# Four GNN layers over 64 graphs: row sums by way of DRAM, natural unit order, other weight loads first, variance groups of four slots

## The chip, the core and the metric

The kernel runs on one core of a Trainium2 chip. The metric is the device time of one execution, in microseconds; the median of three runs stands for a kernel. The engines are named as in the profile: PE (TensorE matmul; PEld is its weight load), DVE (VectorE), ACT (ScalarE), POOL (GpSimd) and SP, whose queue issues all DMAs here.

## The reference

There are 64 graphs of 128 nodes with 128 features, each with a dense 128x128 adjacency matrix, and four GNN layers with a layer norm after each. The cost is in the first layer, which makes a hidden vector for every pair of nodes:

```python
hi = einsum('bsh,hk->bsk', x, W1[:H]); hj = einsum('bsh,hk->bsk', x, W1[H:])
h = relu(hi[:, :, None, :] + hj[:, None, :, :] + b1)      # 128 x 128 pairs of 128 values a graph
y = einsum('bijk,kl->bijl', h, W2) + b2
y = layernorm(y) * gamma + beta                           # over the last axis, for every pair
out = einsum('bij,bijh->bih', adj, y)
...
x = _layernorm(x + L0(x, adj)); x = _layernorm(x + L1(x, adj))
x = _layernorm(x + L2(x, adj)); x = _layernorm(x + L3(x, adj))   # L3 has three such layers inside
```

## The kernel before

**Units and slots.** For a node i, the unit i is the 128x128 tile of h for all j (features on partitions). A graph has 128 units, worked on eight at a time: a slot (16 a graph). Each engine's program is one long list by slots; between its own steps of the first layer it carries the later layers of older graphs (the tail), placed by a table `AT` of slot and ninth of a slot (lines 88 to 101). Engines meet only through semaphores. An engine runs its list in order, so a wait holds all that stands behind it. A stage named with lag L does slot t of a graph in program slot t + L.

**The first layer.** ACT, POOL and DVE make the units of slot t at lag 4 (`START`): `hidden`, lines 556, 924 and 669. POOL makes two units of a slot, or three in the slots of `ROOTLESS`; DVE one in every second slot and four in the last; ACT the rest, five or so. The units go to a ring `h` of 18 slots. PE multiplies the eight units by W2 less its mean in two blocks of 512 columns (`products`, line 417, lag 5), into two PSUM buffers in turn. ACT squares the result (`squares`, line 566, lag 6) into a ring `sq` of four slots. PE sums the squares over the features by matmuls with a one-hot column into `ss_ps` (`variances`, line 429): once in two slots, four matmuls of 512 columns, one to each quarter of 32 output columns. Each fp32 matmul shows as two records. After eight slots ACT takes the square root (`deviations`, line 573), SP's DMAs straighten the rows (line 324), DVE inverts them (693) and multiplies by the adjacency values (`coefficients`, line 701), which also gives a row sum in `c_row_sum`. The coefficients go to DRAM (335) and come back copied to all partitions (347, 349). DVE then sums each unit of h weighted with them (`weighted_sum`, line 685, a custom operation and a read of its accumulator, lag 19), 14 slots behind the products.

**Row sums.** The first layer adds for each node the sum of its coefficients times a bias. The two columns of `c_row_sum` hold half rows in an order of units that groups them by quarter (`unit_of`, line 75). DVE copies them (869), PE brings them to node order with two one-column matmuls against the matrices `row_pick` (`c_sum_mm`, line 450), and DVE copies the result (740), used at line 744.

**Norms.** DVE takes mean and variance (709, 712), POOL adds eps and raises to the power -0.5 (912, 915), DVE applies it (718 or 792) six ninths of a slot after the variance.

**Loads.** SP loads x, then seven weights counted on one semaphore `weights_in`, in the order W1 (two halves), b1, W2, b2 twice, gamma. ACT, DVE and PE wait for all seven. PE starts `make_uv` (402, 403), from which all units come, after DVE has centred W2 and made the affine terms (808 to 821). In each graph SP issues eight DMAs of 32 partitions for `adj_c` (288), then the tail's inputs (358, 359).

## Time and profile before

| | us |
|---|---|
| median of 3 runs (2756.32 to 2757.82) | 2756.94 |
| the profiled execution | 2755.1 |
| its span, first to last instruction | 2753.5 |

PE is busy for 98% of the span, DVE 95%, ACT 93%, POOL 90%. The granted clock of TensorE is at full speed in all slices but the last (nine tenths or more against five), where only the tail is left. A graph takes some 41.9 us in the long middle part. Since all four engines are near full, the busy share alone doesn't tell which sets the pace; the waits and the timeline do. In the profile an instruction's duration includes its way through the pipeline, so neighbours overlap: what a step costs an engine is read from start to start.

### The profile page before, as it was taken

To read this page: it belongs to the slowest core of one execution; us is meant where nothing else is said; L and a number is where in the kernel's file an instruction comes from. 1 tells how busy PE (TensorE), PEld (TensorE's weight loads), DVE (VectorE), ACT (ScalarE), POOL (GpSimd) and SP (SyncE) were. 2 spreads that over 40 slices of the span, in tenths; PEclk is the share of its full clock that TensorE was granted. 3 is DMA by queue.
4 is the path that set the end of the run, shared out by engine and by line. 5 is a ranking of instruction groups with operands and counts; after the bars stand their busy time and mean duration, and the time that the engine had idled before them with its cause. 6 is when DMAs were issued, how large, how long until landed. Compare 5 with 4: busy or idle time off the path is not lost.

```text
span 2753.5 us, 60836 instructions
## 1 busy us (share of the span) xinstructions
PE 2690.3 (98%) x10882; PEld 1147.3 (42%) x10882; DVE 2619.0 (95%) x20102; ACT 2567.7 (93%) x6903; POOL 2487.8 (90%) x3498
## 2 busy tenths in 40 slices
PE   8999999999999999999999999999999999999993
PEld 2344444444444444444444444444444444444442
DVE  4999999999999999999999999999999999999997
ACT  7999999999999999999999999999999999999991
POOL 3899999999999999999999999999999999999992
PEclk9999999999999999999999999999999999999995
DMA  3655655655555555556556555555655565565562
GB/s 108 237 196 209 231 206 196 231 219 194 215 231 201 202 226 219 197 215 231 199 200 232 214 194 221 227 199 203 230 213 197 214 236 196 202 234 210 195 228 95
DMA packets 188668, 571.72 MB, mean 208 GB/s; under 512 B 70656, under 2 KB 106368, under 8 KB 139136
## 3 DMA queue, kind: packets, MB, share of 16 engines
q1 hardware_dynamic: 188288, 567.83, 54.5%
q14 instruction: 285, 2.33, 0.3%
q8 instruction: 95, 1.56, 0.2%
HBM read 555.17 MB, written 8.39 MB: 205 GB/s over the span
## 4 chain that ended last, share of the span: by engine, by line
PE 67%; ACT 18%; DVE 8%; issue 6%; POOL 1%; DMA 0%; SPq 0%; ACTq 0%; DVEq 0%; POOLq 0%
PE y_ps L417 47%; PE ss_ps L429 13%; ACT h L556 11%; DVE h L685 5%; ACT sq L566 4%; ACT dev_rows L573 2%; PE prod_bank L479 1%; PE prod_bank L483 1%; PE prod_bank L450 1%; ACT hid L595 1%; PE prod_bank L456 1%; PE prod_bank L457 1%; PE uv_ps L402 1%; PE uv_ps L403 1%; POOL h L924 1%
## 5 line engine op out<-in xcount | busy, mean ns | idle before, releaser
L924 POOL TENSOR_SCALAR h<-vT,uT 128x128 f32<-128x128 f32 x2520 | 2056.7, 831 | 23.7 <-ACT vT L546 23.3
L417 PE MATMUL y_ps<-h,w2c 128*128 128x512 f32 x4096 | 2016.4, 609 | 11.4 <-DVE h L669 1.6
L685 DVE CUSTOM_DVE_ANT_0 h<-h,cb 128x128 f32<-128x128 f32 x8192 | 1983.9, 289 | 10.0 <-DVE gT_keep L749 0.5
L556 ACT ACTIVATE h<-uv_ps,uT 128x128 f32<-128x128 f32 x4848 | 1409.2, 433 | 0.0
L566 ACT ACTIVATE sq<-y_ps,b2c_col 128x1024 f32<-128x1024 f32 x1024 | 1182.5, 1155 | 112.3 <-PE y_ps L417 112.1
L417 PEld LDWEIGHTS y_ps<-h,w2c 128*128 128x128 f32 x4096 | 682.2, 190 | 903.6 <-issue 723.7
L685 DVE DVE_READ_ACCUMULATOR2_ANT gT<- 128x1 f32 x8192 | 636.8, 78 | 0.1
L429 PE MATMUL ss_ps<-sq,sel 128*32 128x512 f32 x4096 | 545.5, 605 | 0.9 <-ACT sq L566 0.9
L915 POOL TENSOR_TENSOR rs<-var_eps,minus_half 128x1 f32<-128x1 f32 x448 | 302.7, 676 | 35.1
L669 DVE TENSOR_SCALAR h<-vT,uT 128x128 f32<-128x128 f32 x757 | 200.9, 294 | 4.7 <-ACT mask_all L611 2.6
L912 POOL TENSOR_TENSOR var_eps<-mv,eps_col 128x1 f32<-128x1 f32 x448 | 96.1, 215 | 117.9 <-DVE mv L712 115.0
L429 PEld LDWEIGHTS ss_ps<-sq,sel 128*32 128x32 f32 x4096 | 80.6, 108 | 225.5 <-ACT sq L566 105.0
L709 DVE BATCH_NORM_STATS2 stats<-z 128x6 f32<-128x128 f32 x448 | 127.4, 284 | 0.3
L483 PEld LDWEIGHTS prod_bank<-l3w,aggT 128*128 128x128 f32 x384 | 73.6, 194 | 93.0 <-issue 58.6
L693 DVE RECIPROCAL invs<-devs 128x64 f32<-128x64 f32 x128 | 70.1, 548 | 38.6 <-DMA devs<-dev_rows 35.6
L718 DVE TENSOR_SCALAR x<-z,mv,rs 128x128 f32<-128x128 f32 x256 | 96.7, 378 | 6.2 <-POOL rs L915 4.8
L907 POOL TENSOR_TENSOR dis_raw<-degree_floor,minus_half 128x1 f32<-128x1 f32 x64 | 35.1, 548 | 65.3 <-DVE degree_floor L733 65.3
L599 ACT ACTIVATE aggT<-prod_bank 128x128 f32<-128x128 f32 x192 | 66.3, 345 | 25.3 <-PE prod_bank L479 21.7
L604 ACT ACTIVATE h<-z_aff 128x128 f32<-128x128 f32 x192 | 70.4, 367 | 17.5 <-DVE z_aff L792 17.5
L792 DVE SCALAR_TENSOR_TENSOR z_aff<-z_aff,rs,l3beta 128x128 f32<-128x128 f32 x192 | 81.9, 427 | 4.6 <-POOL rs L915 2.9
L573 ACT ACTIVATE dev_rows<-ss_ps 128x512 f32<-128x512 f32 x128 | 79.8, 624 | 1.2 <-PE ss_ps L429 1.2
L712 DVE BATCH_NORM_AGGREGATE mv<-stats 128x2 f32<-128x6 f32 x448 | 77.8, 174 | 2.6
(100 smaller groups left out, 1489.8 us busy)
## 6 DMA issues: line engine op xcount, KB each, us to landing
cb<-c_scratch SPq DMA_DIRECT2D x384, 1024.0 KB, 9.3
cb<-c_scratch SPq DMA_DIRECT2D x256, 512.0 KB, 4.8
adj_c<-in_adj_dram SPq DMA_DIRECT2D x512, 8.0 KB
devs<-dev_rows SPq DMA_DIRECT2D x512, 8.0 KB
x_in<-in_x_dram SPq DMA_DIRECT2D x64, 64.0 KB, 10.8
c_scratch<-c SPq DMA_DIRECT2D x128, 32.0 KB, 1.5
adj_in<-in_adj_dram SPq DMA_DIRECT2D x64, 64.0 KB, 4.4
x_res<-in_x_dram SPq DMA_DIRECT2D x64, 64.0 KB, 5.4
```

What stands on the lines that cost most here:

```text
L417: op = pe.matmul(y_ps[:, t % 2, c0:c0 + COLS], w2c[:], h[:, (SLOTS * g + t) % H_RING, c0:c0 + COLS], start=True, stop=True)
L429: mm = pe.matmul(ss_ps[32 * q:32 * q + 32, :], sel[:, ROWS - 1 - p:ROWS - 1 - p + 32], sq[:, (t + q // 2) % SQ_RING, c0:c0 + COLS], start= ...
L483: pe.matmul(out, aggT[:, b, :], l3w[:, i, :], start=True, stop=False)
L556: op = act.activation(h[:, (SLOTS * g + t) % H_RING, n * P:(n + 1) * P], v, ACT.Relu, bias=uT[:, b, i:i + 1])
L566: act.activation(sq[:, t % SQ_RING, :], y_ps[:, t % 2, :], ACT.Square, bias=b2c_col[:], scale=float(P) ** -0.5).then_inc(sq_done, 1)
L573: act.activation(dev_rows[:, half, :], ss_ps[:], ACT.Sqrt, bias=EPS).then_inc(dev_done, 1)
L669: op = dve.tensor_scalar(h[:, (SLOTS * g + t) % H_RING, n * P:(n + 1) * P], vT[:, b, :], uT[:, b, i:i + 1], 0.0, ALU.add, ALU.max)
L685: op = dve.tensor_tensor_reduce(h[:, (SLOTS * g + t) % H_RING, cols], h[:, (SLOTS * g + t) % H_RING, cols], cb[:, t // 2, c0:c0 + P], 1.0, ...
L709: dve.bn_stats(stats[:, b, :], z[:, b, :]).then_inc(stats_set[name], 1)
L718: dve.tensor_scalar(dst[:, b, :], z[:, b, :], mv[:, b, 0:1], rs[:, b:b + 1], ALU.subtract, ALU.mult).then_inc(normed[name], 1)
L915: pool.tensor_tensor(rs[:, b:b + 1], var_eps[:, b:b + 1], minus_half[:], ALU.pow).then_inc(rs_set[name], 1)
L924: op = pool.tensor_scalar(h[:, (SLOTS * g + t) % H_RING, n * P:(n + 1) * P], vT[:, b, :], uT[:, b, i:i + 1], 0.0, ALU.add, ALU.max)
```

## The change

1. **Natural order.** `unit_of` becomes `8 t + n`. The adjacency values of a half are then one contiguous piece, loaded with one DMA of 128 partitions instead of four of 32.
2. **Row sums through DRAM.** After each store of coefficients SP stores the half's `c_row_sum` (4 bytes a partition) to DRAM, and `load_row_sums` brings both halves back as pairs `c_pair`, of which DVE adds the two. The copy at 869, `row_pick` and the matmuls at 450 go.
3. **Variance groups.** `variances` runs once in four slots with 8 matmuls; `sq` has five slots. `products` moves from one to two slots behind the units (lag 6), squares to lag 7, variances to lag 10, sums to lag 20, and `h` has 19 slots. The tail's steps move by about a slot; `l0_sum` stands two ninths later against `l0_mm`.
4. **POOL.** `ROOTLESS` has nine slots: POOL makes 41 units a graph instead of 40, ACT 76 instead of 77.
5. **Start.** W2 is loaded first, with a semaphore of its own, then W1 and b1 with `w1_in`; PE waits for these alone, and DVE's work on b2 and gamma moves behind its first four units. PE's waits for the later weights' set-up move two slots on.
6. **Last graph.** Its norms no longer use POOL: ACT takes the root of variance plus eps, DVE the reciprocal.

```diff
-TTR_LAG = START + 15
-H_RING = 18
+PRODUCT_LAG = START + 2
+TTR_LAG = START + 16
+H_RING = 19
-SQ_RING = 4
-ROOTLESS = (1, 2, 3, 5, 7, 9, 11, 14)
+SQ_RING = 5
+GROUP = 4
+ROOTLESS = (1, 2, 3, 4, 5, 8, 10, 12, 15)
...
-    half, b = t // HALF, 2 * (t % HALF) + n // BLOCK_UNITS
-    return 64 * half + 16 * (b % 4) + 4 * (b // 4) + n % BLOCK_UNITS
+    return DUO_UNITS * t + n
...
-    ("g_keep", 3, 4), ("l0_mm", 4, 0), ("l0_sum", 4, 5), ("ln0", 4, 6), ("x1_scaled", 5, 6),
+    ("g_keep", 4, 4), ("l0_mm", 5, 0), ("l0_sum", 5, 7), ("ln0", 5, 8), ("x1_scaled", 6, 7),
...
             def load_adj_c_rows(a):
-                rows = a.rearrange("(h q p n) (l j) -> h p q (n l) j", h=2, q=4, p=CHUNKS, l=2)
+                rows = a.rearrange("(h i) (l j) -> h (i l) j", h=2, l=2)
                 for half in range(2):
-                    for p in range(CHUNKS):
-                        sp.dma_start(adj_c[32 * p:32 * p + 32, half, :], rows[half, p]).then_inc(adj_c_in, 16)
+                    sp.dma_start(adj_c[:, half, :], rows[half]).then_inc(adj_c_in, 16)
...
+                wait_apart(sp, c_pair_in, 16 * g)
+                wait_apart(sp, rows_stored[half], 16 * g)
+                sp.dma_start(rows_dram[half].rearrange("(p o) -> p o", o=1), c_row_sum[:, half:half + 1]
+                             ).then_inc(rows_stored[half], 16)
+
+            def load_row_sums(g, b):
+
+                for half in range(2):
+                    wait_apart(sp, rows_stored[half], 16 * (g + 1))
+                wait_apart(sp, c_sum_set, g - 1)
+                wait_apart(sp, c_pair_in, 16 * g)
+                sp.dma_start(c_pair[:, b, :], rows_dram.rearrange("h (i l) -> (h i) l", l=2)).then_inc(c_pair_in, 16)
...
                     spread_coefficients(old, 1)
+                    load_row_sums(old, 1 - buf)
...
             def variances(g, t):
 
-                half, p = t // HALF, (t % HALF) // 2
-                wait(pe, sq_done, SLOTS * g + t + 2)
-                if p == 0:
+                half = t // HALF
+                wait(pe, sq_done, SLOTS * g + t + GROUP)
+                if t % HALF == 0:
                     wait(pe, dev_done, 2 * g + half)
-                for q in range(4):
-                    c0 = (q % 2) * COLS
-                    mm = pe.matmul(ss_ps[32 * q:32 * q + 32, :], sel[:, ROWS - 1 - p:ROWS - 1 - p + 32],
-                                   sq[:, (t + q // 2) % SQ_RING, c0:c0 + COLS],
-                                   start=(p == 0), stop=(p == ROWS - 1))
+                for d in range(GROUP):
+                    p = (t + d) % HALF // 2
+                    for block in range(2):
+                        q = 2 * (d % 2) + block
+                        mm = pe.matmul(ss_ps[32 * q:32 * q + 32, :], sel[:, ROWS - 1 - p:ROWS - 1 - p + 32],
+                                       sq[:, (SLOTS * g + t + d) % SQ_RING, block * COLS:(block + 1) * COLS],
+                                       start=(p == 0), stop=(p == ROWS - 1))
                 mm.then_inc(var_summed, 1)
...
-                if due("c_sum_mm"):
-                    wait(pe, rows_kept, g + 1)
-                    wait(pe, adjT_set, g + 1)
-                    for half in range(2):
-                        op = pe.matmul(c_sum_ps[b], row_pick[:, half, :], rows_sum[:, half:half + 1],
-                                       start=(half == 0), stop=(half == 1))
-                    op.then_inc(c_summed, 1)
...
-            pe.wait_ge(weights_in, 16 * WEIGHTS)
-            pe.wait_ge(w2c_set, 1)
-            pe.wait_ge(affine_set, 2)
+            pe.wait_ge(w1_in, 16 * FIRST_WEIGHTS)
...
-                    sg, t = lagging(graphs, s, START + 3)
-                    if s % 2 == 1 and sg is not None:
+                    sg, t = lagging(graphs, s, PRODUCT_LAG + GROUP)
+                    if t % GROUP == 0 and sg is not None:
                         variances(sg, t)
...
+                for name in NORMS:
+                    if g == G - 1 and lo <= AT[name] + 2 < hi:
+                        wait(act, mv_set[name], g + 1)
+                        act.activation(var_eps[:, b:b + 1], mv[:, b, 1:2], ACT.Sqrt, bias=EPS).then_inc(eps_added[name], 1)
...
+                if g == G - 1 and lo <= at + NORM_AT - 1 < hi:
+                    wait(dve, eps_added[name], g + 1)
+                    dve.reciprocal(rs[:, b:b + 1], var_eps[:, b:b + 1]).then_inc(rs_set[name], 1)
...
-                        if ct == HALF + 1 and cg is not None and k == FINE - 1:
-                            wait(dve, c_made, 2 * (cg + 1))
-                            wait(dve, c_summed, cg)
-                            dve.tensor_copy(rows_sum[:], c_row_sum[:]).then_inc(rows_kept, 1)
```

**On PE**, in a graph of the long middle part, from the row sums to the first layer's end (`y_ps` is a product block, `ss_ps` a variance matmul, `x4` or `x8` how many stand in a row, `uv_ps` the two matmuls of `make_uv`). Before:

```order
L417 MATMUL y_ps<-h,w2c 128x512 x3
L450 MATMUL prod_bank<-rows_sum,row_pick 128x1 x2
L429 MATMUL ss_ps<-sq,sel 32x512 x4
L417 MATMUL y_ps<-h,w2c 128x512 x3
L402 MATMUL uv_ps<-xT,w1a 128x128
L403 MATMUL uv_ps<-xT,w1b 128x128
L417 MATMUL y_ps<-h,w2c 128x512
L429 MATMUL ss_ps<-sq,sel 32x512 x4
```

Now:

```order
L438 MATMUL y_ps<-h,w2c 128x512 x5
L452 MATMUL ss_ps<-sq,sel 32x512 x8
L438 MATMUL y_ps<-h,w2c 128x512
L421 MATMUL uv_ps<-xT,w1a 128x128
L422 MATMUL uv_ps<-xT,w1b 128x128
L438 MATMUL y_ps<-h,w2c 128x512 x4
L472 MATMUL prod_bank<-w2cg,gT_keep 128x128
```

Two groups of four have become one of eight, with one product block between it and `uv_ps` instead of three, and the row-sum matmuls are gone.

**On SP's queue**, from the store of the second half's coefficients to the tail's inputs (`c_scratch` is the store, `cb` the copies to all partitions). Before:

```order
L335 DMA c_scratch<-c 128x64 [waits cb_in7,cb_in6,cb_first1,cb_in5,c_stored1,cb_in4,c_made]
L347 DMA cb<-c_scratch 128x1024 [waits ttr_done,c_stored1]
L349 DMA cb<-c_scratch 128x1024
L349 DMA cb<-c_scratch 128x2048 [waits ttr_done] x3
L288 DMA adj_c<-in_adj_dram 32x1x64 [waits adj_c_in,c_made]
L288 DMA adj_c<-in_adj_dram 32x1x64 x7
L358 DMA adj_in<-in_adj_dram 128x128 [waits x_base_set,tail_in,degree_set,l3_agged2]
```

Now:

```order
L341 DMA c_scratch<-c 128x64 [waits cb_in7,cb_in6,cb_first1,cb_in5,c_stored1,cb_in4,c_made]
L345 DMA row_sum_scratch<-c_row_sum 128x1 [waits rows_stored1,c_pair_in]
L365 DMA cb<-c_scratch 128x1024 [waits ttr_done,c_stored1]
L367 DMA cb<-c_scratch 128x1024
L367 DMA cb<-c_scratch 128x2048 [waits ttr_done] x3
L354 DMA c_pair<-row_sum_scratch 128x2 [waits c_sum_set,c_pair_in,rows_stored1,rows_stored0]
L290 DMA adj_c<-in_adj_dram 128x64 [waits adj_c_in,c_made]
L290 DMA adj_c<-in_adj_dram 128x64
L376 DMA adj_in<-in_adj_dram 128x128 [waits x_base_set,tail_in,degree_set,l3_agged2]
```

A small store stands ahead of the copies, a small load behind them, and six of eight `adj_c` issues are gone.

## Rows read from the trace of the kernel before

**Rows 1.** busy time of each engine over the whole span:

```profile
PE 2690.3 (98%) x10882; PEld 1147.3 (42%) x10882; DVE 2619.0 (95%) x20102; ACT 2567.7 (93%) x6903; POOL 2487.8 (90%) x3498
```

**Rows 2.** the chain of waits that ended last, shares of the span by line:

```profile
PE y_ps L417 47%; PE ss_ps L429 13%; ACT h L556 11%; DVE h L685 5%; ACT sq L566 4%; ACT dev_rows L573 2%; PE prod_bank L479 1%; PE prod_bank L483 1%; PE prod_bank L450 1%; ACT hid L595 1%; PE prod_bank L456 1%; PE prod_bank L457 1%; PE uv_ps L402 1%; PE uv_ps L403 1%; POOL h L924 1%
```

**Rows 3.** busy us of PE, PEld, DVE, ACT, POOL in fifty graphs:

```profile
507.06:2600.11 2093.05, 2087.41 (x8501) 891.02 (x8500) 2031.58 (x15652) 2004.34 (x5401) 1963.56 (x2751) 1.00 0.56 213
```

**Rows 4.** waits in those fifty graphs: us in total, times, longest us:

```profile
PEld y_ps L417 <- ACT h L556: 121.1, 350, 0.4
ACT sq L566 <- PE y_ps L417: 85.7, 200, 0.7
DVE z L753 <- PE prod_bank L457: 32.8, 49, 0.8
DVE invs L693 <- DMA devs<-dev_rows: 8.4, 31, 1.4
```

**Rows 5.** timeline of DVE: start us, duration us, instruction:

```profile
89.21 0.31 DVE L749 COPY gT_keep<-gT 128x128 f32<-128x128 f32 x1
...
507.06 0.31 DVE L749 COPY gT_keep<-gT 128x128 f32<-128x128 f32 x1
...
2600.11 0.31 DVE L749 COPY gT_keep<-gT 128x128 f32<-128x128 f32 x1
...
2683.65 0.31 DVE L749 COPY gT_keep<-gT 128x128 f32<-128x128 f32 x1
```

**Rows 6.** timeline of PE around a variance group and the next:

```profile
1408.51 1.06 PE L429 MATMUL ss_ps<-sq,sel 128*32 128x512 f32 x8
1409.51 1.98 PE L417 MATMUL y_ps<-h,w2c 128*128 128x512 f32 x4
1411.33 0.27 PE L395 MATMUL prod_bank<-ident,x_in 128*128 128x128 f32 x1
1411.44 1.88 PE L417 MATMUL y_ps<-h,w2c 128*128 128x512 f32 x4
1413.16 0.38 PE L479 MATMUL prod_bank<-adj_in,x 128*128 128x128 f32 x2
1413.47 1.06 PE L429 MATMUL ss_ps<-sq,sel 128*32 128x512 f32 x8
```

**Rows 7.** timeline of PE at the row-sum matmuls:

```profile
1423.40 0.50 PE L450 MATMUL prod_bank<-rows_sum,row_pick 128*128 128x1 f32 x4
1423.83 1.07 PE L429 MATMUL ss_ps<-sq,sel 128*32 128x512 f32 x8
```

**Rows 8.** costliest lines, whole span: operation, count | busy us, mean ns | idle:

```profile
L924 POOL TENSOR_SCALAR h<-vT,uT 128x128 f32<-128x128 f32 x2520 | 2056.7, 831 | 23.7 <-ACT vT L546 23.3
...
L685 DVE CUSTOM_DVE_ANT_0 h<-h,cb 128x128 f32<-128x128 f32 x8192 | 1983.9, 289 | 10.0 <-DVE gT_keep L749 0.5
```

**Rows 9.** the same view of DVE alone, 2708 to 2720 us:

```profile
L685 DVE CUSTOM_DVE_ANT_0 h<-h,cb 128x128 f32<-128x128 f32 x47 | 10.7, 282 | 0.0
```

**Rows 10.** timeline of SP's queue and DVE, from row-sum source to its use:

```profile
1405.01 5.37 SPq L288 DMA_DIRECT2D adj_c<-in_adj_dram  x8
...
1424.24 0.08 DVE L685 DVE_READ_ACCUMULATOR2_ANT gT<- 128x1 f32 x1
```

**Rows 11.** timeline of the start:

```profile
2.58 0.43 SPq L297 DMA_DIRECT2D w<-in_L_gnn_W_dram  x1
...
9.38 0.77 PE L402 MATMUL uv_ps<-xT,w1a 128*128 128x128 f32 x2 [6.17 <-DVE b2cg L821]
```

**Rows 12.** DMA issues: size of one, median us from issue to landing:

```profile
b_col<-in_L_gnn_b_dram SPq DMA_DIRECT2D x2, 0.5 KB, 2.8
```

**Rows 13.** timeline of a layer norm in the last graph's tail:

```profile
2727.62 0.18 DVE L712 BATCH_NORM_AGGREGATE mv<-stats 128x2 f32<-128x6 f32 x1
...
2727.88 0.19 POOL L912 TENSOR_TENSOR var_eps<-mv,eps_col 128x1 f32<-128x1 f32 x1 [1.71 <-DVE mv L712]
...
2728.73 0.34 DVE L718 TENSOR_SCALAR x<-z,mv,rs 128x128 f32<-128x128 f32 x1 [0.93 <-POOL rs L915]
```

100 lines of the change are left out of this document (54 added, 46 removed), and 16 rows, old and new, of the table AT.

## The prediction

> **What bounds the kernel now.** I read the busy shares first, then the chain of waits, then the waits and the timeline of fifty graphs from the middle. PE is busy for 98% of the span [rows 1], and the chain that ended last lies for 47% on the products and 13% on the variance matmuls [rows 2]. A graph takes (2600.11 - 507.06) / 50 = 41.86 us, and the same over all 62 steps from the first copy of `gT` to the last but one, (2683.65 - 89.21) / 62 = 41.85 [rows 5]. In these fifty graphs PE shows 2087.41 us busy of 2093.05, DVE 2031.58, ACT 2004.34, POOL 1963.56 [rows 3]: a graph costs PE 41.75 us, DVE 40.63, ACT 40.09, POOL 39.27. ACT's idle time is nearly all waiting for a product, 85.7 us or 1.7 a graph; the weight loads of PE wait 121.1 us for units of ACT, but mostly while the matmul before still streams [rows 4]. So PE sets the pace, with some coupling to ACT, and DVE is right behind it. DVE's two large waits, for `z` (32.8 us) and for the deviations (8.4), are 0.82 us a graph [rows 4]. Without them DVE would need 41.86 - 0.82 = 41.04 us. That is the wall behind PE: whatever PE gains beyond 0.8 us a graph is lost unless DVE gains too.
>
> **Variance groups.** A group starts at 1408.51 and the next product at 1409.51, 1.00 us; eight records over four quarters of the columns are two steps of about 0.43 (four products in a row take 1413.16 - 1411.44 = 1.72), so 0.14 of it is start and end. The four product matmuls behind the group take 1411.33 - 1409.51 = 1.82, 0.10 more than the others. Ahead of the group two short matmuls take 0.31 (1413.16 to 1413.47); I take 0.09 of this as the switch to quarters, an estimate [rows 6]. Each group thus costs 0.33 us beside its streaming. Four of eight per graph go, if the second half of a doubled group streams straight on: 1.3 us less on PE. If it doesn't, only the switches go, 4 x 0.19 = 0.8. If the two halves cost as now and more waits come, nothing.
>
> **Row sums.** PE's two matmuls hold it from 1423.40 to 1423.83, 0.43 us [rows 7]; without them the group's own 0.09 comes back, so 0.34 less. PE then needs 41.75 - 1.3 - 0.3 = 40.1 us a graph and drops under DVE. DVE loses one small copy; the similar one at 740 lasts 0.15 us [rows 10], of which I count 0.1. The other becomes an addition of the same size, no change. The load of the pairs is issued where the `adj_c` loads start now, at 1405.01, and its sum is used at about 1424.24: 19 us of cover [rows 10] against 2.8 us for the landing of a like column [rows 12], plus what the copies ahead of it take. If the cover failed, DVE would stand for the excess and all sums behind it. The small store ahead of the copies takes SP one issue, 0.43 us by the nearest [rows 11], and the copies wait for the coefficients' landing beside it anyway. I price it at 0, with 0.4 us a half as its bound, which the three slots from coefficients to first sum would cover. Two `adj_c` issues instead of eight free the queue of about 4 us out of 5.37 [rows 10], worth nothing, since the tail's loads are not waited for.
>
> **Units and lags.** ACT gives one unit a graph to POOL: 0.43 us long on ACT at most, 0.83 on POOL [rows 8], which then needs 39.27 + 0.83 = 40.1 of its 41. The second slot between units and products takes away PE's waits for ACT's last unit. It does not loosen the loop between products and squares, with only two buffers in PSUM; the doubled group sits in it (a rival below). Products and sums move together, 14 slots apart as before, so the end of the first layer after the last product stays; one more slot of units ahead of products at the start costs up to a slot, 41.85 / 16 = 2.6 us, but ACT is idle there. I take +1. `l0_sum` gets two more ninths of a slot, which takes off most of the 32.8 us.
>
> **Start.** PE now starts `make_uv` at 9.38 us, after all seven weights and DVE's set-up. In the new order b1 is the fifth issue, where one starts at 2.58 now [rows 11], and such a column lands 2.8 us later [rows 12]: 5.4 us. So -4.0, all on the path since nothing else can start. The bound is 0, if POOL's set-up, which waits for the later weights, takes the lead in the second graph.
>
> **Last graph.** From the start of the variance operation to its use in a norm it is 2728.73 - 2727.62 = 1.11 us, with two POOL operations of 0.19 and 0.55 between [rows 13]. One column on ACT and one on DVE I estimate at 0.25 and 0.15, and with hand-offs as here 0.76 in all. Seven norms save 7 x 0.35 = 2.4; some overlap with another graph's, so -2 (0 to -3.5).
>
> **The sum.** Against the profiled execution (2755.1, span 2753.5, 1.6 around it): DVE as the new bound at 41.04 - 0.1 = 40.9, plus 0.1 of waits that stay, makes 41.0 us a graph. 62 x (41.85 - 41.0) = 53 less; -4 start, +1 lag, -2 tail: -58, so 2697 for that execution. It stands 1.8 under the median, so 2756.9 - 58 = **2699**.
>
> **A rule against it.** At the same time in which POOL's units run, DVE's sums last 289 ns on average [rows 8]; with POOL nearly idle at the end they last 282 [rows 9]. All of POOL's 40 units cost DVE's 128 sums 128 x 7 ns = 0.9 us, so one more costs 0.02. DVE at 97% and POOL at 94% busy together [rows 3] leave no room for turns. The Trainium skill's page "SBUF — State Buffer", section "SBUF: two separate sides", says that a VectorE operation with two SBUF inputs and a GpSimd operation that reads SBUF hold one port pair in turn, each blocked for the whole of the other; the trace does not agree for these. If POOL's added unit held DVE up for its full 0.83 us, DVE would need 40.9 + 0.8 = 41.7 and the graphs would gain 9 us at most, which with the ends gives 2743: a chance of 3%.
>
> **Rivals.**
> (a) *The loop of products and squares* takes the place of the bound. From the end of the square that a group waits for: group 1.9 with its switch, next product block 1.82 plus 0.2 to 0.4 of tail matmuls and 0.15 for the last one's end [rows 6], then ACT three squares and two rounds of five units, 3 x 1.0 + 2 x 1.4 (estimates from 40.09 / 16 = 2.5 us a slot, rows 3). That is 9.9 to 10.1 us for four slots, against 10.25 at 41.0 a graph. Nearly level: jitter can take it to 10.35, 41.4 a graph, 62 x 0.45 + 5 = 33 less, **2724**. The same time comes out if POOL, with 0.9 us of slack left, is late with a norm's factor and DVE waits for it. For it speaks that all four engines would be within 1 us of each other; against it that ACT has 1.7 us of waiting to give and the tail matmuls behind three of the four groups are one or none. Chance 23%.
> (b) *Slower*: the same loop, with a doubled group that restarts between its halves (2.1 with the switch) and a square that is late behind ACT's square root of the deviations in two of four groups. The loop exceeds 10.46 us, at which nothing is gained; at 10.6 a graph takes 42.3, 62 x 0.45 = 28 more, less 5: **2780**. It decides from 0.4 us over my sum for the loop. Chance 8%.
> (c) *The groups give only the switches, or the waits move to `z`*: 41.7 a graph, 62 x 0.15 + 5 = 14 less, or the loop just cancels the rest: **2743 to 2755**. Chance 8%, half of it within 0.2%. That the row sums come late and cancel the gain is in here too, at 1%.
> (d) *DVE gains too*: many of its gaps under 0.15 us, 0.4 us a graph in all (61.5 us of idle time in rows 3 less the 41.2 of rows 4, over 50), are short waits for a PE that is late. With PE ahead they go: 40.6 a graph, 62 x 0.4 = 25 less than forecast, **2674**. Chance 13%.
>
> **How the numbers follow.** Forecast 45% (2685 to 2712), (a) 23%, (d) 13%, (b) 8%, (c) 8%, the port rule 3%. The range leaves out (b), the upper end of (c) and the outermost of (d): 2676 to 2744. Faster by over 0.2% (about what a measurement here can tell from no change), under 2751: 45 + 23 + 13 + 3 + half of (c) = 0.87, of which I keep 0.86. Within 0.2%: 0.05. Slower: 0.09.
>
> **What would show it.** Right: `gT` copies 41.0 us apart; DVE busy over 98% in the middle with its wait for `z` at 753 nearly gone; a variance group of 16 records about 1.85 us long; PE's weight loads without waits for ACT's units; the first product at about 8.2 us; `c_pair` never waited for. ACT's waits for products fewer but longer, behind groups. Wrong: groups over 2.0 us long, DVE idle over 1 us a graph on `prod_bank` or POOL's `rs`, or ACT waiting over 2 us a graph for products.

## The result and the profile after

| | us |
|---|---|
| the kernel before, median in the same comparison | 2757.2 |
| the changed kernel, median of 4 runs (3389.52 to 3405.39) | 3401.9 |
| ratio, with its 95% interval | 1.233 (1.231 to 1.235) |
| the profiled execution of after / its span | 3404.1 / 3402.3 |

The forecast was 2699, with 2676 to 2744 as its range. The change makes the kernel 23% slower, by 645 us. One execution of all runs below, of e19, was slow (6088.7 us, where its other three took 2707.6 to 2709.4); e19's time is the median of those three.

Busy time of each engine over the whole span of after, which answers to [rows 1]:

```profile
PE 2904.3 (85%) x10626; PEld 1213.7 (36%) x10626; DVE 2583.3 (76%) x20042; ACT 2569.7 (76%) x6847; POOL 2500.3 (73%) x3547
```

The chain of waits that ended last, by engine and by line, against [rows 2]:

```profile
DMA 48%; DVE 36%; PE 8%; SPq 4%; issue 3%; ACT 1%; DVEq 0%; POOL 0%; ACTq 0%
DMA cb<-c_scratch 33%; DVE h L709 22%; DMA x_res<-in_x_dram 11%; DMA c_scratch<-c 4%; PE y_ps L438 3%; PE ss_ps L452 3%; SPq L367 2%; DVE gT L709 2%; DVE stats L733 2%; DVE z_aff L820 1%; DVE h L693 1%; DVE z_aff L815 1%; DVE z L807 1%; DVE invs L717 1%; SPq L290 1%
```

No engine is near full, and DVE, ACT and POOL have about the same work as before. The chain has gone from PE to a DMA: a third of it is `cb<-c_scratch`, the copy of the coefficients to all partitions; another 11% is the load of the tail's `x_res`, which lands in 10.4 us instead of 5.4. The weighted sums (line 709 now, 685 before), among the costliest lines, against [rows 8]:

```profile
L709 DVE CUSTOM_DVE_ANT_0 h<-h,cb 128x128 f32<-128x128 f32 x8192 | 1975.9, 289 | 669.8 <-DMA cb<-c_scratch 669.3
```

An operation lasts 289 ns, as before, but DVE stands 669 us waiting for the copies, against 10.0 us of idle time before these operations in [rows 8]. That is as long as the whole loss, 10.5 us a graph. The copies' own rows (KB each, median us from issue to landing) in after:

```profile
cb<-c_scratch SPq DMA_DIRECT2D x384, 1024.0 KB, 14.3
cb<-c_scratch SPq DMA_DIRECT2D x256, 512.0 KB, 11.9
```

and in the kernel before:

```profile
cb<-c_scratch SPq DMA_DIRECT2D x384, 1024.0 KB, 9.3
cb<-c_scratch SPq DMA_DIRECT2D x256, 512.0 KB, 4.8
```

The same copies land 5 to 7 us later. SP's queue shows what stands ahead of them. After, one half of a graph (start us, duration us, instruction; 341 stores the coefficients, 345 is the new store of the row sums, 365 and 367 issue the copies):

```profile
1538.98 0.33 SPq L341 DMA_DIRECT2D c_scratch<-c  x1
1539.40 0.38 SPq L345 DMA_DIRECT2D row_sum_scratch<-c_row_sum  x1
1540.45 0.32 SPq L365 DMA_DIRECT2D cb<-c_scratch  x1
1540.82 9.21 SPq L367 DMA_DIRECT2D cb<-c_scratch  x4
```

The same view of the kernel before:

```profile
1400.01 0.32 SPq L335 DMA_DIRECT2D c_scratch<-c  x1
1401.50 0.33 SPq L347 DMA_DIRECT2D cb<-c_scratch  x1
1401.88 3.03 SPq L349 DMA_DIRECT2D cb<-c_scratch  x4
```

In both the first copy is issued 1.5 us behind the store of the coefficients, once that has landed (in after 1.4 us in the median; a single one took 5.7). What is late is the first copy's own landing, first after (line 365), then before (line 347):

```profile
DMA to landing us min/median/max: 6.8/11.3/12.5
DMA to landing us min/median/max: 3.7/4.0/5.4
```

The four copies behind it take 9.21 us to issue instead of 3.03, but that follows from the delay in good part: SP waits for DVE's sums to free the buffers. Its waits for them, after and before (us in total, times, longest):

```profile
SPq L367 <- DVE gT L709: 580.8, 184, 5.5
SPq L349 <- DVE gT L685: 20.3, 69, 0.6
```

On DVE's side of the half shown:

```profile
1552.11 0.29 DVE L709 CUSTOM_DVE_ANT_0 h<-h,cb 128x128 f32<-128x128 f32 x1 [5.41 <-DMA cb<-c_scratch]
```

Fifty graphs in the middle of after, between two copies of `gT` (first the us; then busy us of PE, PEld, DVE, ACT, POOL; the granted clock as a share of full speed; DMA share; GB/s), against [rows 3]:

```profile
614.11:3220.19 2606.08, 2260.13 (x8304) 943.82 (x8302) 2003.36 (x15601) 2005.69 (x5356) 1977.72 (x2801) 0.91 0.61 171
```

A graph takes 52.12 us instead of 41.86. The granted clock is 0.91, where it was 1.00: TensorE's clock spends part of the time at the lower of its two levels, 1.2 instead of 2.4 GHz, while PE now stands idle in every graph, which it did not before. PE's busy time grows from 2087 to 2260 us, but PE still has over 300 us to spare, and DVE's wait for the copies is as long as the loss, so I take the clock as a consequence; no run changes it alone.

### The profile page after: what moved, and what is told of

It is laid out like the page before. It is cut to its first block, busy times and chain, and to the rows that moved or that the text cites. A ratio compares the mean times of both kernels' runs of the same rounds, so it can differ in the third digit from the quotient of the medians.

```text
span 3402.3 us, 60251 instructions
## 1 busy us (share of the span) xinstructions
PE 2904.3 (85%) x10626; PEld 1213.7 (36%) x10626; DVE 2583.3 (76%) x20042; ACT 2569.7 (76%) x6847; POOL 2500.3 (73%) x3547
## 4 chain that ended last, share of the span: by engine, by line
DMA 48%; DVE 36%; PE 8%; SPq 4%; issue 3%; ACT 1%; DVEq 0%; POOL 0%; ACTq 0%
DMA cb<-c_scratch 33%; DVE h L709 22%; DMA x_res<-in_x_dram 11%; DMA c_scratch<-c 4%; PE y_ps L438 3%; PE ss_ps L452 3%; SPq L367 2%; DVE gT L709 2%; DVE stats L733 2%; DVE z_aff L820 1%; DVE h L693 1%; DVE z_aff L815 1%; DVE z L807 1%; DVE invs L717 1%; SPq L290 1%
## 5 line engine op out<-in xcount | busy, mean ns | idle before, releaser
L438 PE MATMUL y_ps<-h,w2c 128*128 128x512 f32 x4096 | 2125.0, 643 | 70.1 <-DVE h L693 60.8
L438 PEld LDWEIGHTS y_ps<-h,w2c 128*128 128x128 f32 x4096 | 748.7, 205 | 958.3 <-issue 733.4
L452 PE MATMUL ss_ps<-sq,sel 128*32 128x512 f32 x4096 | 572.9, 683 | 1.4 <-ACT sq L587 1.2
L495 PE MATMUL prod_bank<-adj_in,x 128*128 128x128 f32 x128 | 40.9, 412 | 228.9 <-DVE x L746 228.9
L452 PEld LDWEIGHTS ss_ps<-sq,sel 128*32 128x32 f32 x4096 | 115.3, 117 | 306.2 <-issue 189.3
L477 PE MATMUL prod_bank<-adjT,x1s 128*128 128x128 f32 x128 | 45.3, 451 | 155.5 <-DVE x1s L787 155.5
L613 ACT ACTIVATE aggT<-prod_bank 128x128 f32<-128x128 f32 x64 | 17.8, 278 | 188.4 <-PE prod_bank L477 188.4
L495 PEld LDWEIGHTS prod_bank<-adj_in,x 128*128 128x128 f32 x128 | 25.3, 247 | 281.0 <-DVE x L746 281.0
L477 PEld LDWEIGHTS prod_bank<-adjT,x1s 128*128 128x128 f32 x128 | 28.1, 274 | 209.2 <-DVE x1s L787 209.2
L499 PE MATMUL prod_bank<-l3w,aggT 128*128 128x128 f32 x384 | 83.6, 300 | 3.5 <-ACT aggT L624 3.4
## 6 DMA issues: line engine op xcount, KB each, us to landing
cb<-c_scratch SPq DMA_DIRECT2D x384, 1024.0 KB, 14.3
cb<-c_scratch SPq DMA_DIRECT2D x256, 512.0 KB, 11.9
adj_c<-in_adj_dram SPq DMA_DIRECT2D x128, 32.0 KB, 10.4
x_res<-in_x_dram SPq DMA_DIRECT2D x64, 64.0 KB, 10.4
```

Of the source, the lines that this page charges most:

```text
L438: op = pe.matmul(y_ps[:, t % 2, c0:c0 + COLS], w2c[:], h[:, (SLOTS * g + t) % H_RING, c0:c0 + COLS], start=True, stop=True)
L452: mm = pe.matmul(ss_ps[32 * q:32 * q + 32, :], sel[:, ROWS - 1 - p:ROWS - 1 - p + 32], sq[:, (SLOTS * g + t + d) % SQ_RING, block * COLS:( ...
L499: pe.matmul(out, aggT[:, b, :], l3w[:, i, :], start=True, stop=False)
```

## The experiments

Times are medians; ratios are against the kernel before on the same chip, with 95% intervals. A graph's time is taken from the first copy of `gT` to the last but one, over 62. The diffs are against the kernel named ahead of them and cut to their core.

### What makes the copies late

**e1, row sums on PE.** The changed kernel with its row sums made as before, by two one-column matmuls (with a `row_pick` for the natural order), and nothing sent through DRAM.

```diff
-                sp.dma_start(rows_dram[half].rearrange("(p o) -> p o", o=1), c_row_sum[:, half:half + 1]
-                             ).then_inc(rows_stored[half], 16)
...
+                if due("c_sum_mm"):
+                    wait(pe, rows_kept, g + 1)
...
+                        op = pe.matmul(c_sum_ps[b], row_pick[:, half, :], rows_sum[:, half:half + 1],
+                                       start=(half == 0), stop=(half == 1))
```

> The changed kernel with the row sums made as before (a copy on VectorE, two one-column matmuls against a pick matrix in natural order, a copy back) and no row-sum DMAs; all else of the change stays. Theory S (the small stores): the 4-byte stores of the row sums hold back the copies of the coefficients by about 5 us twice a graph, and nothing else is slow. Then this run loses the whole of it and shows what the rest of the change is worth, by my forecast less the 0.3 us a graph of the two matmuls, which are back on PE: 2699 to 2720 us, and VectorE's wait for the copies is under 10 us in all instead of 669. Rival G (the groups): the bursts of eight variance matmuls or the new order of loads of the adjacency values are the cause; then it stays over 3200 us.

Measured: 2786.2, ratio 1.011 (1.009 to 1.013), 42.51 us a graph. The way through DRAM costs 616 of the 645 us. But what is left isn't 2699 to 2720: there is a second loss, beyond what this run was expected to show.

**e2, the stores alone.** The kernel before with nothing added but a 4-byte store per partition and half, right behind the store of the coefficients. Nobody reads what is stored. DVE also waits for the previous graph's store before it overwrites the column; e8 below has the same wait.

```diff
+        rows_dram = nc.dram_tensor("row_sum_scratch", (2, P), F32, kind="Internal").ap()
...
                 sp.dma_start(c_dram[half].rearrange("(b j) -> b j", j=SPAN), c[:, half, :]
                              ).then_inc(c_stored[half], 16)
+                wait_apart(sp, rows_stored[half], 16 * g)
+                sp.dma_start(rows_dram[half].rearrange("(p o) -> p o", o=1), c_row_sum[:, half:half + 1]
+                             ).then_inc(rows_stored[half], 16)
```

> The kernel before with one thing added: the store of the half's row sums (128 rows of 4 bytes) to DRAM behind each store of coefficients; nothing reads it. Theory S: about 5 us twice a graph, less the slack of the copies in the kernel before (their wait was 0.5 us in all, so the slack is unknown): 3250 to 3400 us. Rival G: 2757 to 2765 us, since one more issue on SP's queue costs nothing.

Measured: 3358.0, ratio 1.219 (1.216 to 1.221), 51.26 us a graph. Its waits (us in total, times, longest) and the landing of its copies:

```profile
DVE h L692 <- DMA cb<-c_scratch: 639.7, 136, 6.3
```

```profile
cb<-c_scratch SPq DMA_DIRECT2D x384, 1024.0 KB, 14.1
cb<-c_scratch SPq DMA_DIRECT2D x256, 512.0 KB, 11.9
```

Two stores of 512 bytes a graph, in a kernel otherwise unchanged, cost 603 us, 4.7 us each, with the same late copies. Neither the load of the pairs, the natural order nor the lags are needed for it.

**e3, the stores behind the copies.** In the changed kernel each store of row sums is issued behind the half's copies.

```diff
                     spread_coefficients(old, 0)
+                    store_row_sums(old, 0)
...
                     spread_coefficients(old, 1)
+                    store_row_sums(old, 1)
                     load_row_sums(old, 1 - buf)
```

> The changed kernel with the row-sum stores moved behind the copies of the same half on SP's queue; same DMAs, other order. Theory S, in the form that the stores only hold up what stands behind them: the copies of the coefficients run as before, only the loads of the adjacency values and of the tail come about 5 us later, with 19 us of cover: 2690 to 2760 us. In the form that the stores disturb all reads in flight, the copies that are still running are slowed: 2900 to 3400 us. Rival G: 3400 us.

Measured: 3201.3, ratio 1.162 (1.159 to 1.164), 48.82 us a graph. That lies in the range given for the second form of S, but its mechanism is not there: the copies land as in the kernel before (9.3 and 4.8 us). The first form, that only what stands behind the stores is late, fits what follows, but the delay is far over the 5 us that it took. The landing of the stores, SP's longest wait, and one of DVE's:

```profile
row_sum_scratch<-c_row_sum SPq DMA_DIRECT2D x128, 0.5 KB, 14.7
```

```profile
SPq L245 <- DMA row_sum_scratch<-c_row_sum: 910.0, 64, 15.6
```

```profile
DVE degree L761 <- DMA x_res<-in_x_dram: 367.3, 64, 9.1
```

SP stands 14.2 us a graph for the store's landing before it can load the pairs; the next graph's `adj_c` and the tail's loads are issued behind that, and DVE waits 5.7 us a graph for the tail's `x_res`. The slow store now hurts whoever is queued behind it. Putting it elsewhere in the queue moves the bill and doesn't pay it.

**e4, 512 bytes apart.** The changed kernel, each row sum at its own 512 bytes of DRAM.

```diff
-        rows_dram = nc.dram_tensor("row_sum_scratch", (2, P), F32, kind="Internal").ap()
+        rows_dram = nc.dram_tensor("row_sum_scratch", (2, P, P), F32, kind="Internal").ap()
```

> The changed kernel with each row sum stored 512 bytes from the next in DRAM (and gathered from there), so no two of the 4-byte writes share a 512-byte piece. Theory S with many writes to the same piece of memory as the cause: the delay goes, 2690 to 2800 us. Theory S with small writes as such as the cause: 3300 to 3450 us, as now. Rival G: 3400 us.

Measured: 2782.0, ratio 1.010 (1.008 to 1.012), 42.43 us a graph. The same 128 values in the same place of the queue now land in

```profile
row_sum_scratch<-c_row_sum SPq DMA_DIRECT2D x128, 0.5 KB, 1.5
```

and the copies in 9.3 and 4.8 us again. 620 us of 645 are gone, with all else as in the change.

**e8, 64 bytes apart.** The run e2 with the unread values 64 bytes apart.

```diff
-        rows_dram = nc.dram_tensor("row_sum_scratch", (2, P), F32, kind="Internal").ap()
+        rows_dram = nc.dram_tensor("row_sum_scratch", (2, P, 16), F32, kind="Internal").ap()
```

> The kernel of the run e2 (before plus the unused row-sum stores) with the 128 values of a store 64 bytes apart in DRAM instead of 4. If the cost comes from many writes to the same 64 bytes: 2755 to 2800 us. If it comes from writes to the same larger piece (512 bytes or more): the copies stay late, though less often, 2900 to 3360 us.

Measured: 2756.2, ratio 1.000 (0.999 to 1.001), 41.85 us a graph. As many DMAs, packets and bytes as in e2, and nothing of its 603 us is left. It isn't the small size of a piece of data that costs, nor the issue; it is that 128 separate 4-byte writes go to neighbouring addresses. The Trainium skill's page "DMA: Bandwidth & Descriptors", section "Specifications", says that transfers under 512 bytes are done by read-modify-write. The trace agrees that such a store can be dear, but the rule alone would charge e2 and e8 alike, and the store of the coefficients, 256 bytes a row, lands in 1.5 us in both. What happens in the memory no run shows, nor what a spacing between 4 and 64 bytes would give.

### What keeps the repaired change slower than before

Without the slow store the change is at 2782 to 2787, 83 to 88 us over the forecast. Two theories: P, that POOL with its 41st unit has become late; L, the loop of products and squares, lengthened by the doubled variance group (rivals (a) and (b)). In e1 the chain lies for 54% on POOL, which speaks for P.

**e5, 40 units for POOL**, and **e6, 38 units**, both as e1 else.

```diff
-ROOTLESS = (1, 2, 3, 4, 5, 8, 10, 12, 15)
+ROOTLESS = (2, 3, 4, 5, 8, 10, 12, 15)
```

```diff
-ROOTLESS = (1, 2, 3, 4, 5, 8, 10, 12, 15)
+ROOTLESS = (3, 5, 8, 10, 12, 15)
```

> The kernel of the run e1 (the change with row sums on PE) with POOL back at 40 units a graph, slot 1 out of the list of slots with three. In e1 the chain that ended last lies 54% on POOL and a graph takes 42.54 us. Theory P (POOL's 41st unit is what still makes it slower than before): a unit of POOL with its gap, 0.87 us a graph, goes: 41.7 us a graph or less, 2725 to 2735 us, and POOL's share of the chain falls under 20%. Rival L (the longer lags or the doubled variance group cost the time, and POOL only waits with the others): 2780 to 2790 us, with another engine in the chain.

> As e5 with 38 units on POOL and 79 on ACT. Theory P: POOL leaves the chain, the next bound is VectorE at 40.9 to 41.0 us a graph or the loop of squares and products with ACT 0.5 us fuller: 2685 to 2715 us. If ACT takes over as the bound, 2720 to 2760. Rival L: 2780 us or more.

Measured: e5 2786.9, ratio 1.011 (1.009 to 1.013), no gain at all; e6 2770.5, 1.005 (1.004 to 1.007), which lies in none of the three ranges expected. In e5 the chain has only changed its engines:

```profile
ACT 34%; DVE 22%; PE 19%; POOL 15%; issue 9%; DMA 0%; SPq 0%; DVEq 0%; POOLq 0%; ACTq 0%
```

So P falls for the 41st unit: POOL's large share in e1 didn't mean that taking it off would help. e6's 16 us are looked at again below. One doubled group on PE's timeline in e5, and on ACT's the square that waits for the product behind it:

```profile
1417.52 1.92 PE L439 MATMUL ss_ps<-sq,sel 128*32 128x512 f32 x16
1419.38 1.98 PE L425 MATMUL y_ps<-h,w2c 128*128 128x512 f32 x4
```

```profile
1418.30 1.56 ACT L570 ACTIVATE h<-uv_ps,uT 128x128 f32<-128x128 f32 x5
1421.40 1.11 ACT L582 ACTIVATE sq<-y_ps,b2c_col 128x1024 f32<-128x1024 f32 x1 [1.53 <-PE y_ps L425]
```

The group holds PE for 1.86 us; the next slot's product is whole only at 1421.4, and ACT, done with its units at 1419.87, stands 1.53 us. A square that is late can then hold a later group. Groups in e6:

```profile
1409.04 1.92 PE L439 MATMUL ss_ps<-sq,sel 128*32 128x512 f32 x16
...
1419.13 1.92 PE L439 MATMUL ss_ps<-sq,sel 128*32 128x512 f32 x16
...
1429.58 1.92 PE L439 MATMUL ss_ps<-sq,sel 128*32 128x512 f32 x16 [0.25 <-ACT sq L582]
...
1440.21 1.92 PE L439 MATMUL ss_ps<-sq,sel 128*32 128x512 f32 x16
```

They are 10.09, 10.45 and 10.63 us apart, and the group behind them starts at 1451.27, 11.06 later. Wanted were 10.25, and rival (a) summed up 9.9 to 10.1; the mean over the run is 42.25 / 4 = 10.56. The spacings differ with the tail's matmuls between them, so the mean counts and not one of them.

**e7, the 41st unit in the kernel before.**

```diff
-ROOTLESS = (1, 2, 3, 5, 7, 9, 11, 14)
+ROOTLESS = (1, 2, 3, 5, 6, 7, 9, 11, 14)
```

> The kernel before with one unit a graph moved from ACT to POOL (slot 6 added to the slots with three), nothing else. Theory P in its plain form: POOL has 2.6 us idle in 41.9, but must be on time for the norms, so the unit costs a part of its 0.87 us: 2770 to 2800 us. If POOL's idle time covers it, 2750 to 2760 us, and it is the new schedule that made POOL's time dear.

Measured: 2756.6, ratio 1.000 (0.999 to 1.001). Free there, as counted.

**e9, groups of two slots.** e5 with the variance matmuls in groups of two slots again; lags, order and tables stay.

```diff
-SQ_RING = 5
-GROUP = 4
+SQ_RING = 4
+GROUP = 2
```

> The kernel of the run e5 (row sums and 40 units as before, products two slots behind the units) with variance groups of two slots and a ring of four squares, as before. Theory B (the loop: square, then the doubled group, then the next products, then squares again, with only two product buffers, is longer than a slot's time allows): with groups of two the loop has 0.9 us less in it, and the second slot of lag takes away PE's waits for ACT's units: 41.3 to 41.9 us a graph, 2710 to 2750 us. Rival L (the longer lags cost the time): 2775 us or more.

Measured: 2748.2, ratio 0.997 (0.996 to 0.999), 41.88 us a graph. The doubled group costs at least 38.7 us at lag two: e9's chain lies for 70% on POOL, so something else holds it there.

**e11 and e12, lag one.** e5 with the lags, rings, table of the tail's steps and `ROOTLESS` of the kernel before, with groups of four (e11) and of two (e12).

```diff
-PRODUCT_LAG = START + 2
-TTR_LAG = START + 16
-H_RING = 19
+PRODUCT_LAG = START + 1
+TTR_LAG = START + 15
+H_RING = 18
...
-ROOTLESS = (2, 3, 4, 5, 8, 10, 12, 15)
+ROOTLESS = (1, 2, 3, 5, 7, 9, 11, 14)
```

> The kernel of the run e5 with the lags, the ring of 18 slots and the table of the tail as before (products one slot behind the units), and variance groups of four. Theory B: the same loop is in it, and a product block waits for ACT's last unit besides: 2785 us or more. Rival L: 2700 to 2750 us.

> Lags and groups as before together: what is left of the change is the natural order, W2 first and the last graph's norms without POOL. Both theories: the two ends only, 6 us at the start (the first copy of gT stands at 83.1 us in e6 against 89.2) and 3 at the end: 2744 to 2750 us.

Measured: e11 2830.7, ratio 1.027 (1.026 to 1.029), 43.16 us a graph; e12 2747.3, 0.997 (0.996 to 0.998), 41.84. So at lag one the doubled group costs 83.4 us. From lag one to lag two, with its tables, 43.8 of it come back (e11 to e5), and with groups of two nothing is gained (e12 to e9, +0.8). The second slot is not alone in these two steps: the tail's steps and `ROOTLESS` change with it, and with them DVE's wait for a norm's factor from POOL, 1.0 us in all in e11 and e12, goes to 65.0 and 63.5 in e5 and e9. What that costs is shown further down.

**e15, half a group.** e5, but each group does only its first 8 of 16 records. This leaves out half of the variance sums; it is there for its time alone. The rhythm of one group in four slots stays, and only its length goes.

```diff
-                for d in range(GROUP):
+                for d in range(GROUP // 2):
```

> The kernel of the run e5 (groups of four slots, two slots of lag) with only the first half of each variance group's matmuls: the deviations are made from half of the slots, all waits, rings and the rhythm of one group in four slots stay. It separates the length of a group from its rhythm. Theory B (the doubled group stands 1.85 us long in the loop of squares and products): with 1.0 us in it the loop is 0.85 us shorter in four slots, up to 3.4 us a graph, so another engine bounds at 41.0 to 41.9 us a graph: 2700 to 2750 us. If it is the waiting once in four slots for a late square that costs, with whatever length: 2775 us or more.

Measured: 2742.8, ratio 0.995 (0.994 to 0.997), 41.85 us a graph. The time falls to the level of e9, though squares are still released once in four slots, so that rhythm can't be what keeps e5 above it. But with the length of a group its work goes too: PE has (2674.1 - 2499.2) / 64 = 2.7 us less to do in a graph, and e15 can't tell the two apart. e9 has all the work in shorter groups and comes to the same graph, so the length it is. Below 41.85 neither run says anything: something else holds both there, and the chain names it, 72% on POOL.

### Row sums and POOL once more

**e13, row sums by DRAM at lag one.** e12 with the change's way through DRAM, values 64 bytes apart.

```diff
-        rows_dram = nc.dram_tensor("row_sum_scratch", (2, P), F32, kind="Internal").ap()
+        rows_dram = nc.dram_tensor("row_sum_scratch", (2, P, 16), F32, kind="Internal").ap()
```

> The kernel of the run e12 with the row sums through DRAM as the change has them, but 64 bytes apart. PE loses its two one-column matmuls, 0.34 us a graph, and sets the pace there: 62 x 0.34 = 21 us less than e12, 2722 to 2732 us. If the stores or loads disturb the copies even so, e12's time or more.

Measured: 2736.7, ratio 0.993 (0.992 to 0.995), 41.67 us a graph: 10.7 us less than e12. Repaired, this part of the change is a gain, half of what I expected (0.17 us a graph instead of 0.34).

**e14, e16 and e17: lag two, groups of two slots, row sums 64 bytes apart**, with 40, 38 and 36 units for POOL. e14 against the changed kernel, then e16 against e14:

```diff
-SQ_RING = 5
-GROUP = 4
-ROOTLESS = (1, 2, 3, 4, 5, 8, 10, 12, 15)
+SQ_RING = 4
+GROUP = 2
+ROOTLESS = (2, 3, 4, 5, 8, 10, 12, 15)
...
-        rows_dram = nc.dram_tensor("row_sum_scratch", (2, P), F32, kind="Internal").ap()
+        rows_dram = nc.dram_tensor("row_sum_scratch", (2, P, 16), F32, kind="Internal").ap()
```

```diff
-ROOTLESS = (2, 3, 4, 5, 8, 10, 12, 15)
+ROOTLESS = (3, 5, 8, 10, 12, 15)
```

e17 has `(3, 8, 10, 15)`.

> The changed kernel with three repairs: row sums 64 bytes apart in DRAM, variance groups of two slots, 40 units on POOL. Against e9 (row sums on PE, 2748 us) PE has 0.34 us less a graph; but e9's chain lies 70% on POOL, so if POOL sets its pace the time stays at 2742 to 2750 us; if PE does, 2725 to 2732.

> As e14 with 38 units on POOL instead of 40. If POOL's time is what is left in e9 and e14 (chain 70% on POOL), two units with their gaps give up to 1.7 us a graph, until VectorE or PE bounds at 41.0 to 41.4: 2695 to 2725 us. If not, as e14 or slower, since ACT has two units more.

> As the run with 38 units of POOL (lag two, groups of two slots, row sums 64 bytes apart in DRAM: 2707), with 36 units on POOL and 92 on ACT. That run's chain was for 94% on PE, so by the theory that POOL held the graphs only above 38 units, nothing more comes: 2704 to 2712, with the chain still on PE. If POOL's lateness still costs something at 38, a part of it comes back here: 2690 to 2703. If ACT, with two more units of 0.43 us each, becomes the bound, 2713 to 2740, and the chain goes to ACT.

| run | POOL's units | us | ratio | us a graph |
|---|---|---|---|---|
| e14 | 40 | 2747.3 | 0.997 (0.996 to 0.998) | 41.92 |
| e16 | 38 | 2707.3 | 0.982 (0.981 to 0.984) | 41.21 |
| e17 | 36 | 2717.6 | 0.986 (0.984 to 0.988) | 41.39 |

The units of POOL in e14 (busy us, mean ns), its chain and a wait of DVE:

```profile
L946 POOL TENSOR_SCALAR h<-vT,uT 128x128 f32<-128x128 f32 x2520 | 2118.6, 856 | 20.0 <-ACT vT L565 20.0
```

```profile
POOL 67%; DVE 20%; issue 4%; PE 3%; DMA 3%; ACT 2%; SPq 1%; DVEq 0%; POOLq 0%; ACTq 0%
```

```profile
DVE x L746 <- POOL rs L937: 63.0, 63, 1.0
```

And in e16 its chain and units:

```profile
PE 94%; DVE 2%; ACT 2%; issue 1%; DMA 0%; SPq 0%; POOL 0%; DVEq 0%; ACTq 0%
PE y_ps L438 67%; PE ss_ps L452 18%; PE prod_bank L499 2%; PE prod_bank L495 2%; DVE h L709 1%; ACT h L575 1%; PE prod_bank L483 1%; ACT sq L587 1%; PE uv_ps L421 1%; PE uv_ps L422 1%; PE prod_bank L472 1%; PE prod_bank L487 1%; PE prod_bank L490 1%; PE prod_bank L473 1%; PE prod_bank L484 1%
```

Two units less on POOL bring 40.0 us. In e14 POOL is busy for 92% of the span and a norm's factor is late all the same: DVE stands 1.0 us in every graph for `rs`, 63.0 us in all, where it is 5.1 in e16 and 4.8 in the kernel before. In e16 the chain is PE from end to end. Two further units off POOL (e17) make it 10.3 us slower: the time is that of the third case of the expectation, ACT as the bound (96% busy over the span, against 95% in e16; ACT makes 81 units there, the expectation's 92 counts DVE's eleven as ACT's), but the chain still lies for 92% on PE, so which of ACT's added work costs it isn't shown.

But e16 also breaks up a row of slots in which POOL makes three units each. What stands in POOL's list ahead of the norm in e14:

```profile
1416.12 13.99 POOL L946 TENSOR_SCALAR h<-vT,uT 128x128 f32<-128x128 f32 x16
1430.08 0.19 POOL L934 TENSOR_TENSOR var_eps<-mv,eps_col 128x1 f32<-128x1 f32 x1
1430.34 0.56 POOL L937 TENSOR_TENSOR rs<-var_eps,minus_half 128x1 f32<-128x1 f32 x1
```

Sixteen units without a break, then the factor. In the changed kernel, with its 41st unit, the row is of 17, and in the kernel before, with its tail's steps and three-unit slots in other places, it is of twelve:

```profile
1422.05 9.84 POOL L924 TENSOR_SCALAR h<-vT,uT 128x128 f32<-128x128 f32 x12
```

Is it the number of units in a graph, or how many stand ahead of the factor?

**e18 and e19, 40 units in other places.** e14, with one three-unit slot moved by one place, and with all of them spread.

```diff
-ROOTLESS = (2, 3, 4, 5, 8, 10, 12, 15)
+ROOTLESS = (2, 3, 4, 6, 8, 10, 12, 15)
```

```diff
-ROOTLESS = (2, 3, 4, 5, 8, 10, 12, 15)
+ROOTLESS = (1, 3, 5, 7, 8, 10, 12, 15)
```

> As the run with 40 units at lag two, groups of two, row sums 64 bytes apart (2747.3), but the slots in which GpSimd makes three units are (2, 3, 4, 6, ...) instead of (2, 3, 4, 5, ...): the same 40 units, one fewer ahead of the norm that stands behind 17 of them (1416.12 to 1430.08 in that run's trace), which is 0.85 us. If the place of the units costs and not their number, most of the wait of 1.0 us a graph for that norm's factor goes: 2707 to 2722. If the number costs, 2745 to 2750.

> The same, with the three-unit slots spread out (1, 3, 5, 7, 8, 10, 12, 15): again 40 units, and no four such slots in a row. If the place costs and not the number, the wait of DVE for that norm's factor (63.0 us in all) falls to that of the run with 38 units (5.1) and the time to 2705 to 2715, since GpSimd's 40 units fit into 41.2 us a graph by their sum (39.9). If the number costs, 2745 to 2750.

Measured: e18 2746.2, ratio 0.997 (0.995 to 0.998), 41.86 us a graph, no gain; e19 2708.4, 0.983 (0.981 to 0.985), 41.23 us a graph. The same wait of DVE in e19, and its chain by engine:

```profile
DVE x L746 <- POOL rs L937: 12.5, 44, 1.0
```

```profile
PE 89%; DVE 4%; DMA 2%; ACT 1%; POOL 1%; issue 1%; SPq 1%; DVEq 0%; ACTq 0%; POOLq 0%
```

It is the place. With as many units as e14, spread, the time is that of e16 within 1.1 us, and POOL is nearly off the chain (1%) at 93% busy. The expectation of e18 was wrong in its premise: it counts 17 units where there are 16, and the move from slot 5 to slot 6 stays within the row. The row ahead of the factor in e18, then in e19:

```profile
1416.08 13.98 POOL L946 TENSOR_SCALAR h<-vT,uT 128x128 f32<-128x128 f32 x16
1393.95 13.04 POOL L946 TENSOR_SCALAR h<-vT,uT 128x128 f32<-128x128 f32 x15
```

So e18 left the row as it was, and its wait is still 63.6 us; it says nothing against the place. In e19 one unit less stands in the row, 0.94 us, and most of the 1.0 us a graph is gone (12.5 us of 63.0 are left); e16 has 14. e16 and e19 both beat the kernel before, e16 by 49 us, and the changed kernel by 695.

This also explains e6, which has the table of e16: DVE's wait for the factor is 17.1 us in it against 65.0 in e5. And it gives the price of the doubled group with most of that wait out of the way: e6 is 63.2 us slower than e16, and some 10.7 of this are the row sums on PE (e12 to e13, at lag one), which leaves some 52 for the group. e9 and e15, at 41.85 to 41.88 us a graph, have the same late factor (63.5 and 62.1 us); that it is what holds them fits e14 to e19, but no run spreads POOL's units in them.

## Why the prediction was wrong, point by point

**Row sums: the step that failed.** "The small store ahead of the copies takes SP one issue ... I price it at 0, with 0.4 us a half as its bound." The issue was right, 0.38 us. What I didn't price is what the store does to the DMAs behind it: it counts for some 4.7 us a half (e2: 603 us in 128 halves), twelve times the bound, and no row of the kernel before shows a store in pieces of 4 bytes. I bounded the cost with the nearest issue where the nearest landing was wanted. "The three slots from coefficients to first sum would cover" 0.4 us, but not this: of the 5 to 7 us by which the copies come late, 4.7 come through. And I gave late row sums 1% as a cause, but thought of the load of the pairs, which was never waited for. The store's victim was another transfer on the critical path. The Trainium skill's read-modify-write rule, named at e8, was not weighed in the prediction; it speaks against a store in pieces of 4 bytes, and would have been worth a rival.

**PE's 0.34 us for the row-sum matmuls** were worth 0.17 (e12 to e13).

**Variance groups.** A doubled group takes 1.86 us to the next product, against 1.85 forecast, so the step "the second half streams straight on" was right. The 1.3 us a graph can't be found in PE's busy time: it falls from 2697.9 us (e9) to 2674.1 (e5), 0.37 a graph. Busy time was a poor base for "PE then needs ... 40.1": PE shows 98% in e9 as well, where the chain lies on POOL. No gain comes out of the run, and the nearest cause is the loop that I put down as rival (a) and (b). My sum for it, 9.9 to 10.1 us for four slots, fits the shortest spacing shown of e6, 10.09; the mean is 10.56, over the 10.46 at which (b) said that nothing is gained. I gave (b) 8%. Its 2780 against 2782.0 (e4) is in part luck: 10.6 for four slots is 42.4 us a graph and not 42.3, which by its own sum is 2786; of its two causes the restart between the halves (2.1 us) isn't there, the square behind the root was not looked at by itself, and e4's time holds POOL's late factor (62.4 us of DVE's waiting) too. The mis-sized term is the margin: I took 0.15 to 0.35 us as enough in a loop through two engines with an in-order list each, and the mean came out some 0.3 over what was wanted. e9 and e15 together show that the length of the group makes the loss, not its rhythm; which wait in the loop adds up to it is not shown.

**Lag two.** "The second slot takes away PE's waits for ACT's last unit" fits what came back with groups of four, 43.8 us with the late factor against it. With groups of two it first gave nothing (e12 to e9); with POOL's units spread and the row sums off PE the graphs come down from 41.67 us at lag one (e13) to 41.23 (e19), 28 us in all.

**POOL: "then needs 40.1 of its 41".** As a sum right: the added unit is free in the kernel before (e7), and 40 units fit into 41.23 us (e19). What I didn't read is the new table's order. Slots 1 to 5 of `ROOTLESS` follow one another, and the tail's steps have moved, so a norm's factor stands behind 17 units in a row, where it was twelve. The second half of rival (a), "POOL is late with a norm's factor and DVE waits for it", is shown by e14, e16 and e19, but by the place of the units and not by the slack; it costs some 39 us (e14 to e19) once the groups are of two slots.

**DVE as the wall at 41.0** was not reached: in e16 and e19, at 41.2, PE holds the chain. The forecast's 41.0 us a graph was near what such edits can give, but with groups of two slots and another table.

**Start.** PE's first product begins at

```profile
7.61 4.79 PE L438 MATMUL y_ps<-h,w2c 128*128 128x512 f32 x7 [1.69 <-DVE h L693]
```

against 8.2 forecast and 12.17 before. The first copy of `gT` stands at 84.09 in e12, which has the new start at the old lags, 5.1 us earlier than in [rows 5], against 4.0 forecast. The added slot of lag, for which I took +1, costs nothing: e9 has that copy at 83.45.

**Last graph.** A norm of its tail in after, against [rows 13]:

```profile
3397.14 0.18 DVE L736 BATCH_NORM_AGGREGATE mv<-stats 128x2 f32<-128x6 f32 x1
3397.36 0.20 ACT L605 ACTIVATE var_eps<-mv 128x1 f32<-128x1 f32 x1 [1.86 <-DVE mv L736]
...
3397.63 0.15 DVE L739 RECIPROCAL rs<-var_eps 128x1 f32<-128x1 f32 x1
3397.89 0.35 DVE L820 SCALAR_TENSOR_TENSOR z_aff<-z_aff,rs,l3beta 128x128 f32<-128x128 f32 x1
```

From the variance to its use it takes 0.75 us, 0.76 forecast. From the last copy of `gT` to the end of the span it is 33.0 us before and 30.3 in e12: 2.7 less, 2 forecast. Natural order, with two loads instead of eight, cost nothing, as said.

**The sum.** The right parts (start, last graph, row sums off PE) are worth 19.1 us of the 58 (e13 against the 2755.7 of before beside it); the groups, forecast as the largest gain, lose 39 (e5 against e9) to some 52; the place of POOL's units loses some 39 where the groups don't hide it; and one store at a price of 0 costs 620 us, ten times the whole gain forecast. Nothing in the range stood for it, since every rival but the 1% for late row sums was about engines, and none about what one DMA does to the next.

## What to carry to other kernels

A store that cuts its data into pieces of a few bytes a partition is priced by its landing, and by what it does to the transfers behind it on the critical path, not by its issue; where the trace has no such piece, its cost is open at the upper side. If it has to be, give each value 64 bytes of its own in DRAM: here that took the cost from 603 us to nothing. And when work is gathered into longer pieces to save switches, sum up the loop that waits for the piece, ask for slack in it (1.5 to 3.5% were not enough here), and read the order of each engine's list as well as its sum: here an engine at 92% held the others with one late result, and at 93% in another order it didn't.
